# Delta rule: the output and the scans of a head moved inside the levels of the head after it, kq_g on GpSimd, one setup block

## What is computed

```
mixed = causal_conv4(layernorm(x) @ qkv_w.T)         # q, k, v: 8 heads of 128
beta  = sigmoid(h @ b_w.T);  alpha = exp(-exp(A_log) * softplus(h @ a_w.T + dt_bias))
for t:                                               # per sequence and head
    S = S * alpha_t
    S = S + outer(k_t, (v_t - k_t @ S) * beta_t)
    o_t = q_t @ S
o = o * rsqrt(mean(o**2) + 1e-6) * norm_w * silu(z)  # z = h @ z_w.T
x = x + o @ out_w.T
```

## Time and profile before

| what | value |
|---|---|
| median of three runs | 4598.96 us (4592.67 to 4600.91) |
| the profiled execution | 4603.23 us, span 4601.5 us |
| busy share of the span | PE 83%, PEld 62%, DVE 60%, ACT 48%, POOL 35% |
| delta stage, from its layer norm to its last add | 2725.9 to 3708.5 us |
| its heads | 2809.0 to 3708.5 us |

### The profile page before, as it was taken

The page is one execution under the profiler, slowest core; times in us unless marked ns, Lnnn a source line. Parts: engine busy times, 40 slices in busy tenths (PEclk is TensorE's granted clock), DMA queues, the critical chain, the costliest instruction groups (busy, mean ns, idle before and its releaser), DMA issues. The chain is left out here.

```text
span 4601.5 us, 120161 instructions
## 1 busy us (share of the span) xinstructions
PE 3818.9 (83%) x48456; PEld 2871.1 (62%) x48456; DVE 2758.2 (60%) x4248; ACT 2203.6 (48%) x4333; POOL 1617.6 (35%) x1493
## 2 busy tenths in 40 slices
PE   4666769989989989989989967888888764667998
PEld 1224458868868858858858844666666762225555
DVE  5895557457457547547547636555555445984554
ACT  4442257557557557557657633333333224442222
POOL 2661057337437437527527502111111102661000
PEclk7988889999999999999999986666666677987999
DMA  0000011011101101101101000000000000001000
GB/s 13 0 0 16 1 50 33 30 29 32 32 27 32 35 25 32 37 23 32 39 23 32 24 1 7 6 6 6 6 6 6 4 5 6 0 0 55 0 0 9
DMA packets 56556, 83.35 MB, mean 18 GB/s; under 512 B 13146, under 2 KB 32628, under 8 KB 54900
## 3 DMA queue, kind: packets, MB, share of 16 engines
q1 hardware_dynamic: 56052, 75.99, 5.5%
HBM read 30.87 MB, written 1.05 MB: 7 GB/s over the span
## 5 line engine op out<-in xcount | busy, mean ns | idle before, releaser
L1759 POOL TENSOR_TENSOR local_rot<-local_term 128x512 f32<-128x512 f32 x384 | 478.9, 1268 | 640.8 <-DVE local_term L2077 640.8
L2077 DVE TENSOR_TENSOR local_term<-bank,local_table 128x512 f32<-128x512 f32 x768 | 485.2, 674 | 108.8 <-ACT local_sq L1965 100.0
L2000 ACT ACTIVATE local_attn<-bank 64x256 f32<-64x256 f32 x768 | 290.9, 379 | 340.4 <-PE bank L1856 333.6
L272 POOL TENSOR_TENSOR mamba_hc<-mamba_state,mamba_c_all 128x512 f32<-128x512 f32 x256 | 319.5, 1270 | 319.4 <-DVE mamba_state L451 314.0
L1765 POOL TENSOR_TENSOR local_rot<-local_rot,local_inv 128x512 f32<-128x512 f32 x384 | 392.7, 1044 | 92.7 <-ACT local_inv L1976 91.2
L1800 PE MATMUL bank<-local_w_layer,local_xs 128*128 128x256 f32 x1536 | 398.2, 404 | 29.0 <-issue 20.5
L1800 PEld LDWEIGHTS bank<-local_w_layer,local_xs 128*128 128x128 f32 x1536 | 286.3, 196 | 82.1 <-issue 32.7
L2138 DVE TENSOR_REDUCE local_most<-bank 128x8 f32<-128x512 f32 x192 | 132.8, 692 | 310.5 <-PE bank L1835 310.5
L1856 PE MATMUL bank<-local_pt,local_v_moved 64*128 64x64 f32 x3072 | 315.0, 283 | 0.0
L1856 PE MATMUL bank<-local_pt,local_v_at 64*128 64x64 f32 x3072 | 305.7, 277 | 0.0
L451 DVE TENSOR_TENSOR_SCAN mamba_state<-bank,mamba_dbu 128x512 f32<-128x512 f32 x256 | 298.4, 1207 | 0.0
(11 more groups left out here) (367 smaller groups left out, 8524.5 us busy)
## 6 DMA issues: line engine op xcount, KB each, us to landing
local_v_moved<-local_v_at SPq DMA_DIRECT2D x192, 192.0 KB, 2.4
local_w_layer<-a_w_layer_dram SPq DMA_DIRECT2D x6, 1536.0 KB, 7.2
local_v_moved<-local_v_at SPq DMA_DIRECT2D x192, 32.0 KB, 2.0
moe_w<-f_w_dram SPq DMA_DIRECT2D x3, 2048.0 KB, 16.3
local_w_o<-a_w_o_dram SPq DMA_DIRECT2D x12, 256.0 KB, 4.0
local_w_up<-a_w_up_dram SPq DMA_DIRECT2D x6, 341.0 KB, 4.7
moe_w<-f_w_dram SPq DMA_DIRECT2D x3, 576.0 KB, 4.6
delta_w_h<-g_w_qkv_dram SPq DMA_DIRECT2D x8, 192.0 KB, 2.4
```

Source lines behind the costliest of these rows:

```text
L272: ins = pool.tensor_tensor(hc[:, b, h, :], state[:, b, h, :], c_all[:, b, :], ALU.mult)
L1759: pool.tensor_tensor(rot[:, i % 2, :, f, :], here[:, :, f, :], there[:, :, 1 - f, :], ALU.add).then_inc(summed, 1)
L2000: ins = act.activation(tokens[ch, v, :, :].rearrange("p k (r q) -> p k r q", r=2), g.bank[6 + v][ch, :].rearrange("p (k r h q) -> p k r h ...
L2077: dve.tensor_tensor(term[:, which, b, :], g.bank[b][:, :], table[:, which, :, :].rearrange("p n c -> p (n c)"), ALU.mult).then_inc(roped, 1)
```

## The change

It does the following:

- **Output of head h inside the levels of head h + 1.** O goes to banks 4 to 7. Its squares are summed for all four quads before one Ln and one Exp (`stat` is laid out anew). ScalarE scales quads 0 and 1 (eight copies of 128x128) and VectorE quads 2 and 3 (`scale_output`, after the four `lt` of the next head) into the new tile `o_n`; GpSimd gates (`gate_output`). TensorE turns quad after quad through bank 2 (`turn_output`) and multiplies through bank 3 (`project_output`), in the slots 17 to 24 of the next head. Head 7's output follows at the end.
- **Values and keys are turned in slots 0 to 3**, values through banks 2 and 3 in turn. Projections take slots 4 to 24, the spread of alpha slots 5, 7, 9, 11, the gates 13, 15, 17, 19. VectorE does all three convolution steps of a projection in the slot after it, and both scans of a quad in the slot after its alpha.
- **kq_g** is made by GpSimd, after its ten masks; its `diagonal` follows directly, into a tile of its own.
- The first products of the solve are put between the products of queries and keys.
- **One setup block.** The inner block is gone. Clearing is GpSimd's, beside the layer norm; head 0's weights are loaded there too. The decays are split into three parts before they are turned, as 96 columns at once. Head 0's projections and convolutions run beside this.
- Head 0 is written out apart from the loop (heads 1 to 6). SyncE loads w_h, wz_h and wo_h each when the head before has used it.

Core of the diff (what only carries new names is left out):

```
+        AT_SLOT = {0: "v0 v1", 1: "k0 k1", 2: "v2 v3", 3: "k2 k3", 4: "p0", 5: "a0", 6: "p1", 7: "a1", 8: "p2", 9: "a2",
+                   10: "p3", 11: "a3 p4", 12: "p5", 13: "z0", 14: "p6", 15: "z1", 16: "p7", 17: "z2 t0", 18: "p8",
+                   19: "z3 t1 o0", 20: "p9", 21: "t2 o1", 22: "p10", 23: "t3 o2", 24: "p11 o3"}
...
         @block.gpsimd
+            def gate_output(h, n):
+                if n < 2:
+                    pool.wait_ge(o_copied, h * 2 + (n + 1))
+                else:
+                    pool.wait_ge(o_scaled, h * 2 + (n - 1))
+                pool.tensor_tensor(o_n[:, n, :, :], o_n[:, n, :, :], sz[:, QUAD * n:QUAD * (n + 1), :], ALU.mult).then_inc(on_ready, 1)
...
+                for n in range(QUADS):
+                    odd = qkv[:, 0:2, tok(n)].rearrange("q m (s p c) -> q m s p c", s=SEQS, p=2)[:, :, :, 1, :]
+                    pool.tensor_tensor(kq_g[:, :, SEQS * n:SEQS * (n + 1), :], odd,
+                                       grow[:, n, :, :].unsqueeze(1).to_broadcast([P, 2, SEQS, C]), ALU.mult).then_inc(kq_ready, 1)
+                if following:
+                    pool.wait_ge(a_ready, h * QUADS + QUADS)
+                    stage_pick(h + 1)
+                    pool.wait_ge(scanned, h * (2 * QUADS) + 2 * QUADS)
+                    stage_beta(Chain(pool, pool_own, h + SETUP), h + 1)
+                    for n in range(QUADS):
+                        diagonal(n)
+                if later(h):
+                    for n in range(QUADS):
+                        gate_output(h - 1, n)
+                    pool.wait_ge(on_ready, h * QUADS)
...
         @block.tensor
+            def turn_output(h, n, free, free_at):
+                pe.wait_ge(on_ready, h * QUADS + (n + 1))
+                if n:
+                    pe.wait_ge(ot_copied, h * QUADS + n)
+                elif free is not None:
+                    pe.wait_ge(free, free_at)
+                for i in range(QUAD):
+                    mm = pe.transpose(chunk(g.bank[2], i), o_n[:, n, i, :], g.ident[:, :])
+                mm.then_inc(ot_ready, 1)
+
+            def project_output(h, n):
+                if n == 0:
+                    pe.wait_ge(wo_loaded, h * 16 + 16)
+                if n:
+                    pe.wait_ge(out_added, h * QUADS + n)
+                pe.wait_ge(ot_copied, h * QUADS + (n + 1))
+                four(g.bank[3], lambda i: chunk(o_t[:, n, :], i), lambda i: wo_h[:, :], out_ready)
...
+                pe.wait_ge(conv_step, h * (PROJ * STEPS) + GROUPS * STEPS)
+                for n in range(QUADS):
+                    four(g.bank[n], lambda i: seg(1, n, i), lambda i: seg(1, n, i), kk_ready)
+                pe.wait_ge(conv_step, h * (PROJ * STEPS) + PROJ * STEPS)
+                pe.wait_ge(a_copied, h * QUADS + QUADS)
+                queries_by_keys(0)
+                queries_by_keys(1)
+                first_products(0)
+                queries_by_keys(2)
+                first_products(1)
+                queries_by_keys(3)
...
         @block.scalar
+                    act.activation(o_sq[:, n, :], g.bank[4 + n][:, :], ACT.Square).then_inc(sq_ready, 1)
+                act.wait_ge(var_ready, h * QUADS + QUADS)
+                act.activation(stat[:, 1, :, :], stat[:, 0, :, :], ACT.Ln, bias=eps_o[:, 0:1], scale=1.0 / P).then_inc(act_own, 1)
+                act.wait_ge(act_own, h * 2 + (OWN + 1))
+                act.activation(stat[:, 2, :, :], stat[:, 1, :, :], ACT.Exp, scale=-0.5).then_inc(act_own, 1)
+                act.wait_ge(act_own, h * 2 + (OWN + 2))
+                act.sem_inc(rstd_ready, 1)
+                for n in range(2):
+                    for i in range(QUAD):
+                        ins = act.activation(o_n[:, n, i, :], chunk(g.bank[4 + n], i), ACT.Copy, scale=stat[:, 2, n, i:i + 1])
+                    ins.then_inc(o_copied, 1)
...
         @block.vector
+                def slot(s):
+
+                    for what, k in items(s - 1, h, following):
+                        if what == "p":
+                            for step in range(STEPS):
+                                convolve(h + 1, k, step)
+                        elif what == "a":
+                            scan_decays(h + 1, k)
+                        elif what == "o":
+                            add_output(h - 1, k)
```

More of the change, by code:

```diff
@@ L1346, in _ @@
+            head(0, True)
+            with pe.Fori(1, HEADS - 1) as h:
                 head(h, True)
             head(HEADS - 1, False)
+            for n in range(QUADS):
+                turn_output(HEADS - 1, n, None, 0)
+                project_output(HEADS - 1, n)
         @block.scalar
@@ L1572, in _ @@
+            own.step(dve.tensor_copy(mid[:, :, :], rest))
+            dve.tensor_tensor(low, rest, mid[:, :, :], ALU.subtract).then_inc(split, 1)
             for i in range(PROJ):
```

620 lines of the change are left out of this document (301 added, 319 removed).

## The result

The changed kernel takes 4468.9 us (median of four executions, 4465.0 to 4484.4) against 4595.8 (4592.1 to 4600.9): ratio 0.9729, 95% interval 0.9704 to 0.9755, 127 us less. The forecast was 112 us less, 4487 us, and the range held the result. The profiled execution took 4470.1 us (span 4468.4).

What follows compares the result with a forecast made beforehand. TensorE was taken as the bound, busy 83% of the span, its levels mostly at half clock. Setup -21, head 0 -20, heads 1 to 6 -76 and head 7 +5 gave -112 us: 4487 us, range 4448 to 4588.

Steps and rivals of the forecast that it cites:

- Setup: Before head 0: one block, bound by VectorE's chain, first masked product at about 2788; gain 21 us (17 to 24).
- The idle stretch: From the last output product to the next head's first key product: TensorE's 16.5 us of waiting go entirely.
- (a): The 16.5 us between last output product and next key product, when TensorE has little to do and other engines work.
- Levels 1 to 4: Solve levels of each head, taking in keys, values and projections 0 to 6: 50 us, against 47 in the trace.
- Levels 32 and 64: Last two levels, with output work slotted in: 37.7 us at half clock, 23 at full, full about three quarters of it.
- Rival 1: Slotted work meets the half clock in every head, 115.5 us a head: 4584 us; chance 0.20.
- Rival 3: Between first key product and level 1 the full clock is lost while TensorE waits: 4668 us; chance 0.07.
- Rival 4: Another engine is late in the levels (kq_g or three convolution steps), 3 to 8 us a head: 4510 to 4540; chance 0.13.
- Rival 2: Clock stays full throughout, levels at the floor of 11 us each, 91 us a head: 4424 us; chance 0.05.
- Head 0: First head, no earlier output to take in: -16.5, and -3.5 before level 1, so -20 us.
- Head 7: Last head, no following head hides its output chain, about 18 us against 13.8: +5 us (0 to +12).
- Contention: VectorE's scans beside GpSimd's diagonals and gating in levels 2 and 3: up to 2.4 us a head, counted as nothing.

Runs made afterwards that it cites:

- e5: The kernel before with only the new setup block, its heads untouched: 4575.4 us, ratio 0.9962.
- e8: e7 with heads 1 to 6 written out one after another instead of looped: 4460.3 us, ratio 0.9695.
- e1: The kernel after with the four kq_g products moved back from GpSimd to VectorE, ahead of level 1: 4470.4 us, ratio 0.9720.
- e7: The kernel after with the last head's slotted output work in slots 6 to 14 and its own output through four banks each: 4463.1 us, ratio 0.9709.
- e6: The kernel before with projections, alpha spreads and gates in the slots of the kernel after, no work added: 4616.2 us, ratio 1.0039.
- e3: The kernel before with unread gate products repeated in slots 17, 19, 21 and 23 of every head: 4619.5 us, ratio 1.0073.
- e9: e6 with unused turnings and products, 16 each a head, in the output work's places in slots 17 to 24: 4604.9 us, ratio 1.0025.
- e2: The kernel after with each head's output gated, turned, multiplied and added at the end of its own head: 4574.0 us, ratio 0.9961.
- e4: The kernel after with output turning, product and adding left out in heads 0 to 6: 4445.4 us, ratio 0.9695.
- e10: The kernel after with the output work in levels 3 and 4 (slots 8 to 15) and gating ahead of GpSimd's diagonals: 4456.2 us, ratio 0.9697.
- e11: e7 with the slots of e10: 4468.7 us, ratio 0.9748.

## Why the prediction was right, and where it was off

**Setup**, forecast -21: -20.1 between the profiles, -19 by e5. The terms of VectorE's chain held, and one that was put at nothing did not. In the kernel after TensorE's and VectorE's queues are (answers to the earlier trace rows):

```profile
2739.78 6.98 PE L1339 MATMUL bank<-delta_w_ab,xnT 128*128 128x16 f32 x32 [1.74 <-PEq L75]
```

```profile
2751.47 2.30 DVE L1508 SCALAR_TENSOR_TENSOR delta_qkv<-bank,delta_taps_h,delta_qkv 128x510 f32<-128x510 f32 x3
2753.68 0.68 DVE L1627 CAST delta_alpha<-bank 96x512 bf16<-96x512 f32 x1
2757.09 15.60 DVE L1508 SCALAR_TENSOR_TENSOR delta_qkv<-bank,delta_taps_h,delta_qkv 128x510 f32<-128x510 f32 x21
2784.35 0.68 DVE L1515 TENSOR_TENSOR_SCAN delta_grow<-delta_alpha_in,delta_alpha_first 128x256 f32<-128x256 f32 x1
2786.18 2.48 DVE L1537 TENSOR_TENSOR delta_lt<-delta_db,bank 128x512 f32<-128x512 f32 x4
```

The split ends at 2751.5 as worked out, the first masked product comes at 2786.2 against 2788 forecast: the waiting of 1.4 us for the turned parts didn't come, as projections stood between. From TensorE's w_ab product to there are 46.4 us against 69.4, 23.0 less. The other 2.9 us were lost ahead of it, in the layer norm, beside which GpSimd now clears buffers, which the prediction counted as no cost. VectorE's smallest step there, before and after:

```profile
2728.58 0.17 DVE L156 TENSOR_SCALAR delta_ln_stats<-delta_ln_stats 128x16 f32<-128x16 f32 x1
```

```profile
2725.91 2.90 DVE L156 TENSOR_SCALAR delta_ln_stats<-delta_ln_stats 128x16 f32<-128x16 f32 x1
```

GpSimd's clearing runs from 2723.4 to 2730.6 without a gap. The step takes 2.90 us in all nine traces that have the new setup and 0.17 in the four that have the old one; no run moves the clearing alone.

**The idle stretch**, forecast -16.5 to nothing: right but for 1.3 us a head. The seams are marked "issue", 1.43 to 1.76 us, where the loop goes round; the unrolled e8 has none. The prediction didn't price the jump, which was hidden in (a) before. The part of it that ScalarE and VectorE used came back in the next term, 9.1 us to level 1 where 10.7 was forecast, so the two together are 10.6 against 10.7.

**Levels 1 to 4**, forecast 50: 50.8 measured. The size is right, the comparison beside it is not: "against 47 in the trace" is the last head's time (46.8), while heads 1 to 6 of before took 50.9. Nothing was added on balance: 24 records of turning came in, one projection and two gates went out.

**Levels 32 and 64**, forecast full clock in three quarters of the heads, 26.7 us: 23.5. This is the term that was mis-sized, by 3 us a head, 19 over six heads, and it outweighs the rest of the miss. Full-clock time was put at 23; the kernel after shows 21.2 and 21.5 in the two heads in which the clock was full throughout, and 24.4 to 24.8 in the four in which the first 8 us or so were still at half. What was wrong is the weight: in all six heads the clock rose. Over the kernels with output work in these slots (after, e1, e7, e8) it was 24 of 24; I had only one head of before to go by the earlier trace rows. Two readings beside it were off without entering the sum: in the trace of before these levels stayed at half in six of the seven heads 0 to 6 and not in five, and the idle stretch (a) was at full clock for only 5 to 6.5 of its 16.5 us.

**Why the clock rises** was argued in the prediction from the density of the slotted work; that the stretches ahead of earlier rises were alike was said there without rows. The runs bear the direction out and correct the reason. Heads 1 to 6 in which the clock rose in levels 32 and 64, one profile each:

| kernel | idle stretch ahead of the head | dense work added in these levels | heads |
|---|---|---|---|
| before, e5 | 16 us | none | 1, 0 of 6 |
| e6 | 16 us | projections later | 0 of 6 |
| e3 | 16 us | 32 records | 4 of 6 |
| e9 | 16 us | 48 records, projections later | 6 of 6 |
| e2 | 21 us | projections later | 3 of 6 |
| e4 | none | projections later | 5 of 6 |
| e10, e11 | none | projections later, output in levels 3 and 4 | 6, 5 of 6 |
| after, e1, e7, e8 | none | projections later, output | 24 of 24 |

So e9 against e6 shows that dense work there is enough, with the idle stretch in place; e4 and e10 show that it isn't needed in these levels where the idle stretch is gone and keys and values are turned in the levels. Neither theory stands alone. The turning of keys and values was never tested without the rest, so whether e4 and e10 owe the clock to it or to the missing idle stretch is open. So is what differs between e2, with the clock risen in half its heads, and e6, with none, and why the same queue of one kernel gets either level from one head to the next. The Trainium skill (TensorE: Matmul & The Clock Gate, "HAM oscillation") has long pauses as what throws the clock back. In e6 there is no pause in these levels, 24.9 us busy of 24.9 at 0.50: the trace shows that the absence of pauses is not enough for the full clock, as it did in the kernel before.

**Rival 1**, half clock with the output in the levels (37.7 us there), came in none of heads 1 to 6. **Rival 3**, the full clock lost between key product and level 1, did not come: these 9 us lie within the stretch 3054 to 3102 at 1.00. **Rival 4**: ScalarE's taps never waited for kq_g (their 161.5 us of waiting in the kernel after ended with TensorE's projections), and e1 shows kq_g worth nothing. Its other half, three convolution steps in a row ahead of an update, is in e6 too, and levels 1 to 4 take 50.9 us there as in the kernel before. **Rival 2** asked for 44 us in levels 1 to 4 at full clock; in the head shown they are at half for 37 of 50 us.

**Head 0**, forecast -20: -16.7. It has no output in its slots and stayed at half in levels 32 and 64, which took 24.9 us against 19.8, and the way from its first masked product to level 1 shrank by 0.9 us and not by 3.5. In e7, e10 and e11 the clock rose in the same head 0, with the same instructions, and these levels took 18.5 us. **Head 7**, forecast +5: +7.4. Its tail grew from 13.8 to 20.8 us where 18 was forecast: 3.77 us a quad was the upper end of the 2.7 to 3.8.

**Contention**: the up to 2.4 us a head that the scans could have cost did not come. All grow scans take 0.68 us in the kernel after and all diagonals 1.04, where in the heads of before three of four scans took 1.46. The rule of the Trainium skill (SBUF — State Buffer, "Who interferes with whom") shows in e1: the masks take 1.17 to 1.24 us while VectorE reads two SBUF operands for kq_g, 0.72 to 0.91 while it doesn't.

## What to carry to other kernels

When an engine waits at the seam of two iterations for a long chain on other engines, give that chain other PSUM banks and move it into the next iteration: here the seam went from 16.3 to 1.3 us, 15.0 of the 15.3 us won a head, while the one move of an operation to another engine that was tested alone, kq_g, was worth nothing. Where the granted clock in the profile's rows goes between its two levels, cost each phase at both and look how often either comes; the average of one profile hides that the same instructions take 17.3 or 24.9 us (e2). Ask also what a cover costs the engine beside it: beside clearing on GpSimd a step of 0.17 us on VectorE took 2.90. Judge versions that differ by less than 0.3% by several executions, for a single profile shows here mainly in how many heads the clock was up.

## What was not expected of the hardware

- Work that nobody needs can shorten a stretch: 284 records took 24.9 us at 0.50, 332 took 22.7 at 0.85 (e6, e9).
- A TensorE that is busy without a gap for 25 us may stay at half clock (e6), and in one with a 21 us chain of waits ahead of the head the clock may rise in the same place (e2, 18.5 us).
- Going round the loop costs TensorE 1.43 to 1.76 us in which it issues nothing; the other engines work on, so that writing the loop out gained 0.6 us a head, which can't be told from nothing.
- A TENSOR_SCALAR of 128x16 on VectorE took 2.90 us instead of 0.17 while GpSimd cleared buffers.
